# A four-layer residual kernel with two convolutions and two mixes: the prologue is rebuilt

## The chip, the cores and the metric

The kernel runs on one core of a Trainium2 chip. The metric is the device time in microseconds; the comparison is between medians of several executions of the kernel before and of the kernel after the change. One execution of each was also recorded by the profiler.

## What is computed

For 32 samples, each x of 128 channels by 2048 positions, and a condition vector of 128 for each sample:

```python
x = x + conv1d(x, w0, groups=4, taps=9, pad=4) + (cond @ ctx0.T)[:, :, None] + side[None, :, None]
for l in (1, 2):
    h = gelu(gelu(cond @ W0 + b0) @ W1 + b1)
    att = softmax(h @ W2 + b2)                      # 8 weights for each sample
    agg_w = einsum('bk,koi->boi', att, weight)      # a 128 x 128 matrix for each sample
    x = x + einsum('boi,bih->boh', agg_w, x) + (att @ bias_k)[:, :, None]
x = x + conv1d(x, w3, groups=4, taps=9, pad=4) + (cond @ ctx3.T)[:, :, None] + side[None, :, None]
```

## The kernel before, in words

The samples are worked on one after the other. A residual layer is a linear map plus the identity, so the identity is added to its weights. The two mixes of a sample are multiplied into one 128 x 128 matrix (`product`), which is applied once (`mix`). What remains for a sample is conv0 (layer 0), mix (layers 1 and 2) and conv3 (layer 3).

The positions of a sample are kept as four planes (`x_planes`: position modulo 4). A convolution is then 12 shifts, and each number is split in two parts (hi and lo) for precision; a shift needs three products: hi by hi, hi by lo, and lo by hi. That gives `TURNS` = 36 turns, and a turn (`conv_turns`, L677) is four matmuls of 32 rows by 512 columns, one for each group, side by side in the array. A mix is 12 such turns. The results of a sample fill four of the eight PSUM banks, and even and odd samples take turns at the halves.

For each sample, ScalarE writes the hi part (`high_x`, `high_y`, `high_z`) and VectorE the lo part (`low_x`, `low_y`, `low_z`). VectorE also sums the eight weights of each mix into the sample's matrices (`mix_matrices`, L526, 16 instructions), and splits their product (`split_product`). SP copies the split product to four places (`spread_mix_w`), loads x (`load_x`), copies the results of conv3 across partitions (`relay_out`) and stores them (`store`). GpSimd interleaves x into planes (`plane_x`) and the planes back into positions (`weave_out`). Order on an engine is that of the program; semaphores are the only waits across engines.

Step t (`one(t)`) does, on TensorE, conv0 of sample t, the first 18 turns of conv3 of sample t-1, the product of sample t+1, the other 18 turns, and the mix of sample t. ALL lists the 33 steps; a hardware loop runs steps 2 to 27 (`LOOP`, L225), the others are written out.

Ahead of the steps stands the prologue. It loads the weights, builds the taps of both convolutions as 128 x 128 matrices (`tap_blocks` on VectorE, L557, nine `tap_matmuls` on TensorE, L749, then `taps_high` and `taps_low`), computes the attention (`hidden`, `gelus`, `logits`, softmax on VectorE and ScalarE), spreads it to a table (`att_tab`), and computes the biases (`conv_biases`, L769, and `mixed_bias`, L762). In it are also conv0 of sample 0 and the first product. conv0 of sample 0 begins when x_lo and the low taps of sample 0 are there:

```python
            pe.wait_ge(taps_lo_done[0], PH)
            conv0(zero, range(MID))
```

Both products of samples 0 and 1 are written to a corner of bank 6, and the second waits behind the mix of 0:

```python
                if t.at(0):
                    product(t, 1)
                    pe.wait_ge(prod_lo_done, 2)
                    pe.wait_ge(taps_lo_done[1], PH)
```

## Time and profile before

| | us |
|---|---|
| median of 3 runs | 716.09 (715.66 to 717.77) |
| the profiled execution | 715.86 |
| its span | 714.1 |
| TensorE busy in the span | 664.8 |

The span is what the profiler sees of the execution, from the first instruction to the last; the profiled execution's own time is 1.8 us more. A time in the rows counts from the span's start. PE is TensorE, DVE VectorE, ACT ScalarE, POOL GpSimd, SP the queue from which most transfers are issued. "L683" is a line of the kernel. A time in square brackets is how long the engine had idled, and what ended that.

### The profile page before, as it was taken

The page shows a single profiled execution, that of the slowest core. Times are in us where ns is not written, and L with a number is a line of the kernel's source. Part 1 is how long each engine was busy: PE and PEld are TensorE (multiplying, and loading weights), DVE is VectorE, ACT ScalarE, POOL GpSimd, SP SyncE. Part 2 cuts the span into 40 slices and gives each one's busy share as a digit, 9 for nine tenths or more (in the row PEclk, how much of TensorE's full clock was granted, in tenths as well). Part 3 has the DMA queues.
Part 4 walks back from the last instruction along what each step waited for, and adds up shares of the span by engine and source line. Part 5 has one row for each costly group of instructions (what it writes and reads, how often), then busy time and mean ns, then how long its engine had stood idle before and what let it go on. Part 6 is the DMA issues. An engine that isn't in the chain of part 4 may idle for free.

```text
span 714.1 us, 24424 instructions
## 1 busy us (share of the span) xinstructions
PE 664.8 (93%) x11104; PEld 650.9 (91%) x11104; DVE 484.8 (68%) x941; ACT 256.5 (36%) x319; POOL 253.5 (36%) x94
## 2 busy tenths in 40 slices
PE   4846999999999999999999999999999999999970
PEld 4645889999999999999999999999999999999960
DVE  5378677767676667776777776787777777777221
ACT  3303433343334443434333444343443344432211
POOL 7022233343344444334334444433433444422220
PEclk9957999999999999999999999999999999999986
DMA  8131478889988888889998888888999888666666
GB/s 274 61 90 31 114 184 194 182 155 206 175 181 187 192 192 190 189 166 176 206 174 182 187 192 191 190 185 163 180 206 180 171 192 194 134 131 128 109 120 152
DMA packets 50238, 119.72 MB, mean 168 GB/s; under 512 B 5865, under 2 KB 25369, under 8 KB 42265
## 3 DMA queue, kind: packets, MB, share of 16 engines
q1 hardware_dynamic: 48592, 118.66, 77.7%
q10 hardware_dynamic: 1352, 0.57, 0.3%
q8 instruction: 22, 0.36, 0.3%
q14 instruction: 16, 0.12, 0.1%
q0 software_dynamic: 256, 0.01, 0.0%
HBM read 35.33 MB, written 33.55 MB: 96 GB/s over the span
## 4 chain that ended last, share of the span: by engine, by line
PE 91%; DVE 3%; DMA 2%; ACT 1%; issue 1%; ACTq 0%; SPq 0%; DVEq 0%
PE ps L683 77%; PE ps L724 12%; DMA out_planes<-in_L_cond_c_weight 1%; DMA out_planes<-out_taps 1%; DVE out_planes L561 1%; DVE acc L540 1%; PE ps L711 1%; PE ps L753 1%; DVE y_lo L503 0%; DVE z_lo L513 0%; DVE mat2T L540 0%; ACT out_sb L411 0%; PE ps L778 0%; DVE mat L540 0%; DVE taps_lo L569 0%
## 5 line engine op out<-in xcount | busy, mean ns | idle before, releaser
L337 POOL COPY out_sb<-out_planes 128x2048 f32<-128x2048 f32 x31 | 122.1, 3939 | 301.2 <-DMA out_planes<-out_taps 301.2
L683 PE MATMUL ps<-z_hi,taps_hi 32*128 32x512 f32 x1536 | 203.8, 402 | 3.6 <-DVE z_lo L513 3.6
L683 PE MATMUL ps<-x_hi,taps_hi 32*128 32x512 f32 x1536 | 202.2, 397 | 1.0 <-DVE prod L553 1.0
L683 PE MATMUL ps<-z_hi,taps_lo 32*128 32x512 f32 x1536 | 201.2, 394 | 0.5 <-issue 0.5
L683 PE MATMUL ps<-x_lo,taps_hi 32*128 32x512 f32 x1536 | 200.9, 394 | 0.0
L683 PE MATMUL ps<-x_hi,taps_lo 32*128 32x512 f32 x1536 | 200.7, 393 | 0.0
L683 PE MATMUL ps<-z_lo,taps_hi 32*128 32x512 f32 x1536 | 200.3, 393 | 0.0
L330 POOL COPY x_planes<-x_in 128x2048 f32<-128x2048 f32 x31 | 120.3, 3881 | 138.9 <-DVE x_lo L496 135.8
L388 ACT ACTIVATE y_hi<-ps,bias_tab 128x512 fp32r<-128x512 f32 x128 | 77.6, 690 | 213.5 <-PE ps L683 213.5
L513 DVE SCALAR_TENSOR_TENSOR z_lo<-ps,bias_tab,z_hi 128x1024 fp32r<-128x1024 f32 x64 | 79.2, 1280 | 74.9 <-ACT z_hi L398 74.9
L683 PEld LDWEIGHTS ps<-z_hi,taps_hi 32*128 32x128 f32 x1536 | 120.8, 186 | 6.1 <-DVE z_lo L513 4.0
L683 PEld LDWEIGHTS ps<-x_hi,taps_hi 32*128 32x128 f32 x1536 | 121.2, 186 | 3.0 <-DVE prod L553 1.2
L683 PEld LDWEIGHTS ps<-x_lo,taps_hi 32*128 32x128 f32 x1536 | 121.4, 187 | 1.7 <-issue 0.2
L683 PEld LDWEIGHTS ps<-x_hi,taps_lo 32*128 32x128 f32 x1536 | 121.3, 186 | 1.7
L683 PEld LDWEIGHTS ps<-z_lo,taps_hi 32*128 32x128 f32 x1536 | 121.1, 186 | 1.1
L683 PEld LDWEIGHTS ps<-z_hi,taps_lo 32*128 32x128 f32 x1536 | 120.6, 185 | 1.3
L503 DVE SCALAR_TENSOR_TENSOR y_lo<-ps,bias_tab,y_hi 128x512 fp32r<-128x512 f32 x128 | 87.3, 745 | 46.8 <-ACT y_hi L388 46.8
L724 PE MATMUL ps<-y_hi,mix_w 32*128 32x512 f32 x1024 | 98.9, 394 | 0.0
L406 ACT ACTIVATE out_taps<-ps,bias_tab 128x512 f32<-128x512 f32 x64 | 40.6, 685 | 155.7 <-PE ps L683 155.7
L398 ACT ACTIVATE z_hi<-ps,bias_tab 128x1024 fp32r<-128x1024 f32 x64 | 67.9, 1113 | 46.7 <-PE ps L724 46.7
L724 PEld LDWEIGHTS ps<-y_hi,mix_w 32*128 32x128 f32 x1024 | 72.8, 186 | 0.8
L496 DVE TENSOR_TENSOR x_lo<-x_planes,x_hi 128x2048 fp32r<-128x2048 f32 x31 | 70.8, 2285 | 0.0
(102 smaller groups left out, 566.2 us busy)
## 6 DMA issues: line engine op xcount, KB each, us to landing
out_planes<-out_taps SPq DMA_DIRECT2D x128, 256.0 KB, 7.4
x_in<-in_x SPq DMA_DIRECT2D x31, 1024.0 KB, 11.0
out<-out_sb SPq DMA_DIRECT2D x31, 1024.0 KB, 4.2
mix_w<-prod SPq DMA_DIRECT2D x128, 128.0 KB, 4.5
x_in<-in_x SPq DMA_DIRECT2D x2, 512.0 KB, 6.1
out<-out_sb SPq DMA_DIRECT2D x2, 512.0 KB, 3.1
out_taps<-in_L_cond_weight SPq DMA_DIRECT2D x1, 512.0 KB, 9.5
mix_w<-in_L_cond_weight SPq DMA_DIRECT2D x1, 512.0 KB, 13.2
```

The costliest lines, as they stand in the source:

```text
L330: pool.tensor_copy(x_planes[:, :, :], x_in[t.par(d)][:, :].rearrange("c (s p) -> c p s", p=PH))\
L337: pool.tensor_copy(out_sb[t.par(d)][:, :].rearrange("c (s p) -> c p s", p=PH), out_planes[:, :, :])\
L388: act.activation(y_hi[:, g, :], ps[:, bank(t, 0) + g, :], ACT.Identity, bias=bias_tab[:, b, g:g + 1]).then_inc(y_hi_done, 1)
L398: act.activation(z_hi[:, 2 * h:2 * h + 2, 1:S + 1], ps[:, k:k + 2, :], ACT.Identity, bias=bias_tab[:, b, 2 * G:BIAS]).then_inc(z_hi_done, 1)
L406: act.activation(out_taps[:, g, :], ps[:, bank(t, d) + g, :], ACT.Identity, bias=bias_tab[:, b, G + g:G + g + 1]).then_inc(out_act, 1)
L496: dve.tensor_tensor(out=x_lo[p][:, :, 1:S + 1], in0=x_planes[:, :, :], in1=x_hi[p][:, :, 1:S + 1].bitcast(F32), op=ALU.subtract).then_inc( ...
L503: dve.scalar_tensor_tensor(out=y_lo[:, g, :], in0=ps[:, bank(t, 0) + g, :], scalar=bias_tab[:, b, g:g + 1], in1=y_hi[:, g, :].bitcast(F32) ...
L513: dve.scalar_tensor_tensor(out=z_lo[:, 2 * h:2 * h + 2, 1:S + 1], in0=ps[:, k:k + 2, :], scalar=bias_tab[:, b, 2 * G:BIAS], in1=z_hi[:, 2 ...
L540: dve.scalar_tensor_tensor(out=o, in0=inputs[0], scalar=att_tab[:, b, K * l + k:K * l + k + 1], in1=inputs[1], op0=ALU.mult, op1=ALU.add). ...
L561: dve.tensor_copy(blocks[rows(g), :, rows(g)], conv_in[l][rows(g), :, :].rearrange("o c t -> o t c"))\
L683: tile = pe.matmul(ps[:, first_bank + g, :], w[rows(g), d, :], a[rows(g), d % PH, d // PH:d // PH + S], start=(n == 0), stop=(n == TURNS - 1))
L724: tile = pe.matmul(ps[:, bank(t, 0) + p, :], w[rows(p), g, h, :], a[rows(p), g, :], start=(n == 0), stop=(n == 3 * G - 1))
```

## The change

It touches only the prologue and the first steps; the arithmetic that gives the output is the same.

- **Loads.** SP issues both halves of x of sample 0 first, then the weights in the order of their use, and the x of sample 1 last. ScalarE issues conv0's taps, cond and four bias rows. The biases and `side` come as five rows and are turned by TensorE together with cond.
- **Taps.** VectorE transposes the taps in 32 x 32 blocks (`turn_taps`); `tap_blocks` and `tap_matmuls` go away. Both `taps_high` and `taps_low` read SBUF.
- **Biases.** The context products are one for each convolution (`contexts`), their result is multiplied with a 0/1 table (`ctx_columns`), and one product for each convolution spreads it. `mixed_bias` sums its eight products in PSUM.
- **First samples.** Samples 0 to 3 are read straight from `x_in`, at every fourth word, without `x_planes` (`PLANED` = 4). Steps 1 to 3 have an order of their own on ScalarE, VectorE, SP and GpSimd (`early`).
- **Turn order.** In every convolution the turns run over the 12 shifts first with hi by hi, then lo taps, then lo data; conv0 waits for x_lo only ahead of turn 24. conv0 of sample 0 is cut into eight pieces with the small products between them.
- **Second product.** conv0 of sample 1 runs around the mix of 0 (22 turns ahead of it, 14 behind); then comes the product of 1, into the banks of z of sample 0, and conv3 of 0 waits for its sum.
- The loop begins at step 4.

```diff
-        LOOP = (1, (N - 4) // 2)
+        LOOP = (2, (N - 4) // 2)
...
-                sp.wait_ge(x_planed, b - 1)
+                if isinstance(b, int) and b - 2 < PLANED:
+                    wait(sp, x_lo_done, b - 1)
+                else:
+                    sp.wait_ge(x_planed, b - 1 - PLANED)
...
+            def early(t):
+                if t.has(-2):
+                    relay_out(t, -2)
+                    load_x(t, 2)
+                    store(t, -2)
+                spread_mix_w(t, 1)
...
-            sp.dma_start(conv_in[0], conv0_w).then_inc(conv_w_in[0], DMA)
             for h in range(2):
                 sp.dma_start(x_in[0][:, h * L // 2:(h + 1) * L // 2], x[0, :, h * L // 2:(h + 1) * L // 2])\
                   .then_inc(x0_halves[h], DMA)
+            for l, m in enumerate((mix1, mix2)):
+                sp.dma_start(mlp_w[l][0], m[0]).then_inc(hidden_w_in[0], DMA)
+            sp.dma_start(mlp_rows[4:5, :], side.rearrange("(a c) -> a c", a=1)).then_inc(mlp_rows_in, DMA)
+            for l, m in enumerate((mix1, mix2)):
+                sp.dma_start(mlp_w[l][1], m[2]).then_inc(hidden_w_in[1], DMA)
+            for l, w in enumerate((ctx0_w, ctx3_w)):
+                sp.dma_start(ctx_in[l], w).then_inc(ctx_w_in[l], DMA)
+            sp.dma_start(conv_in[1], conv3_w).then_inc(conv_w_in[1], DMA)
             sp.dma_start(mix2_in, mix2[6].rearrange("k o i -> o k i")).then_inc(mix2_arrived, DMA)
+            sp.dma_start(mix1_w[:, :, :], mix1[6].rearrange("k o i -> o k i")).then_inc(mix1_arrived, DMA)
             sp.dma_start(x_in[1][:, :], x[1]).then_inc(x_loaded[1], DMA)
-            sp.dma_start(mix1_w[:, :, :], mix1[6].rearrange("k o i -> o k i")).then_inc(mix1_arrived, DMA)
             zero = Step(0, 0)
             load_x(zero, 2)
+            spread_mix_w(zero, 0)
             load_x(zero, 3)
-            spread_mix_w(zero, 0)
-            for t in ALL:
+            spread_mix_w(zero, 1)
+            for t in ALL[1:PLANED]:
+                early(t)
+            load_x(ALL[PLANED - 1], 3)
+            load_x(ALL[PLANED - 1], 4)
+            for t in ALL[PLANED:]:
                 one(t)
...
+            act.wait_ge(x0_halves[0], DMA)
+            act.activation(x_hi[0][:, :, 1:1 + S // 2], planes(x_in[0], half(0)), ACT.Copy).then_inc(x0_high, 1)
             gelus(0)
...
             gelus(1)
+            act.activation(soft[0:1, 41:42], ones[0:1, 0:1], ACT.Exp).then_inc(exp_tables, 1)
+            for p in range(PH):
+                taps_high(1, p)
...
+            def turn_taps(l):
                 dve.wait_ge(conv_w_in[l], DMA)
+                dve.transpose(taps_raw[l][:, :, :], conv_in[l].rearrange("o c t -> o t c")).then_inc(taps_raw_step[l], 1)
+                dve.wait_ge(fold_done, 1)
+                dve.wait_ge(taps_raw_step[l], 1)
+                dve.tensor_tensor(out=taps_raw[l][:, PAD, :], in0=taps_raw[l][:, PAD, :], in1=fold[:, :], op=ALU.add)\
+                   .then_inc(taps_raw_step[l], 1)
...
+            def early(t):
+                if t.at(1):
+                    low_y(t)
+                mix_matrices(t, 1)
+                if not t.at(1):
+                    low_y(t)
+                split_product(t, 1)
+                if t.at(1):
+                    evac_out(t, -1)
+                low_x(t, 1)
+                if not t.at(1):
+                    evac_out(t, -1)
+                low_z(t)
...
+            turn_taps(0)
+            dve.wait_ge(condT_psum, 2)
+            dve.tensor_copy(mlp_col[:, :], ps[:, 6, 0:N + 5]).then_inc(condT_done, 1)
+            dve.wait_ge(halo_done, HALOS)
+            dve.wait_ge(x0_halves[1], DMA)
+            dve.tensor_copy(x_hi[0][:, :, 1 + S // 2:1 + S], planes(x_in[0], half(1))).then_inc(x_hi_done, 1)
+            dve.wait_ge(taps_zeroed, 4)
             for p in range(PH):
                 taps_low(0, p)
+            dve.wait_ge(x0_high, 1)
+            low_x0(0)
+            turn_taps(1)
+            dve.wait_ge(x_hi_done, 1)
+            low_x0(1)
             dve.wait_ge(logits_psum, 1)
...
+            low_x(zero, 1)
+            dve.wait_ge(bias_tab_done, 3)
             low_y(zero)
...
+            mix_matrices(zero, 1)
+            low_z(zero)
+            split_product(zero, 1)
+            for t in ALL[1:PLANED]:
+                early(t)
+            low_x(ALL[PLANED - 1], 2)
+            for t in ALL[PLANED:]:
                 one(t)
...
-                    d, k = n // 3, n % 3
-                    w, a = ((taps_hi[l], hi), (taps_hi[l], lo), (taps_lo[l], hi))[k]
+                    k, d = n // SHIFTS, n % SHIFTS
+                    w, a = ((taps_hi[l], hi), (taps_lo[l], hi), (taps_hi[l], lo))[k]
...
+                if t.at(1):
+                    pe.wait_ge(prod_summed, 2)
...
+            hidden(0)
+            pe.wait_ge(taps_hi_done[0], PH)
+            conv0(zero, range(3))
+            hidden(1)
+            conv0(zero, range(3, 8))
+            logits()
+            conv0(zero, range(8, SHIFTS))
...
+            conv0(zero, range(28, 32))
             pe.wait_ge(agg_done, 1)
             product(zero, 0)
+            conv0(zero, range(32, TURNS))
             mixed_bias()
+
+            pe.wait_ge(bias_tab_done, 3)
+            pe.wait_ge(prod_summed, 1)
+            conv0(first, range(22))
+            mix(zero)
+            conv0(first, range(22, TURNS))
+            product(zero, 1)
+            pe.wait_ge(taps_lo_done[1], PH)
```

## Rows read from the trace of the kernel before

**Rows 1.** The page: the chain of waits, share of each engine.

```profile
PE 91%; DVE 3%; DMA 2%; ACT 1%; issue 1%; ACTq 0%; SPq 0%; DVEq 0%
```

**Rows 2.** Stretches: busy us (x instructions) of each engine, granted clock, DMA share, GB/s.

```profile
17.27:33.40 16.13, 16.13 (x182) 12.77 (x180) 3.60 (x13) 4.13 (x12) 1.63 (x1) 1.00 0.20 75
33.40:64.20 30.80, 12.79 (x87) 11.24 (x86) 23.39 (x58) 9.82 (x12) 3.84 (x1) 0.65 0.18 52
64.20:70.00 5.80, 5.77 (x56) 4.64 (x60) 5.80 (x4) 0.00 (x0) 3.50 (x1) 0.51 0.36 93
107.50:681.30 573.80, 573.80 (x9968) 573.43 (x9961) 410.43 (x791) 217.47 (x260) 215.69 (x56) 1.00 0.85 178
```

**Rows 3.** TensorE's timeline: start, us, line, operation, what it waited for.

```profile
17.27 0.80 PE L683 MATMUL ps<-x_hi,taps_hi 32*128 32x512 f32 x4
...
24.06 1.08 PE L778 MATMUL ps<-out_planes,out_sb 128*128 128x32 f32 x8
...
62.76 0.50 PE L707 MATMUL ps<-mat2T,mat 128*128 128x128 f32 x2 [4.94 <-DVE mat2T L540]
64.23 0.80 PE L683 MATMUL ps<-x_hi,taps_hi 32*128 32x512 f32 x4 [0.97 <-DVE prod L553]
...
75.25 0.42 PE L683 MATMUL ps<-z_hi,taps_hi 32*128 32x512 f32 x4
```

**Rows 4.** VectorE's timeline, same columns.

```profile
8.77 1.08 DVE L604 COPY x_planes<-x_in 128x1024 f32<-128x1024 f32 x1 [1.32 <-DMA x_in<-in_x]
...
20.50 0.68 DVE L630 TENSOR_TENSOR spread<-soft,ident 32x512 f32<-32x512 f32 x1
...
32.66 2.73 DVE L503 SCALAR_TENSOR_TENSOR y_lo<-ps,bias_tab,y_hi 128x512 fp32r<-128x512 f32 x4 [4.28 <-ACT y_hi L388]
35.46 0.35 DVE L540 SCALAR_TENSOR_TENSOR acc<-mix_w,att_tab,ident 128x128 f32<-128x128 f32 x1
...
39.42 0.33 DVE L540 SCALAR_TENSOR_TENSOR mat2T<-mix_wT,att_tab,acc 128x128 f32<-128x128 f32 x1
...
43.95 5.24 DVE L561 COPY out_planes<-out_sb 32x288 f32<-32x288 f32 x4
...
55.99 2.43 DVE L569 TENSOR_TENSOR taps_lo<-ps,taps_hi 128x288 fp32r<-128x288 f32 x4 [5.14 <-ACT taps_hi L417]
...
64.09 2.29 DVE L496 TENSOR_TENSOR x_lo<-x_planes,x_hi 128x2048 fp32r<-128x2048 f32 x1
66.30 2.47 DVE L513 SCALAR_TENSOR_TENSOR z_lo<-ps,bias_tab,z_hi 128x1024 fp32r<-128x1024 f32 x2
...
80.03 0.69 DVE L548 TENSOR_REDUCE prod_sum<-ps 128x128 f32<-128x512 f32 x1 [1.11 <-PE ps L711]
```

**Rows 5.** ScalarE's timeline, same columns.

```profile
18.07 1.28 ACT L474 ACT_TABLE_LOAD   x1
...
53.72 2.25 ACT L417 ACTIVATE taps_hi<-ps 128x288 fp32r<-128x288 f32 x4 [16.59 <-PE ps L753]
...
57.94 2.12 ACT L398 ACTIVATE z_hi<-ps,bias_tab 128x1024 fp32r<-128x1024 f32 x2 [0.26 <-PE ps L724]
```

**Rows 6.** GpSimd's timeline, same columns.

```profile
44.15 3.84 POOL L330 COPY x_planes<-x_in 128x2048 f32<-128x2048 f32 x1 [25.25 <-DVE x_lo L496]
```

**Rows 7.** The page's DMA issues: count, KB each, median us to landing.

```profile
x_in<-in_x SPq DMA_DIRECT2D x31, 1024.0 KB, 11.0
...
mix_w<-prod SPq DMA_DIRECT2D x128, 128.0 KB, 4.5
x_in<-in_x SPq DMA_DIRECT2D x2, 512.0 KB, 6.1
```

**Rows 8.** The chain of waits in order of time: start, us, what.

```profile
98.73 0.46 issue
...
100.38 4.31 PE ps L683 x70
...
147.07 12.58 PE ps L683 x216
```

More of the change, by code:

```diff
@@ L282, in one @@
             def one(t):
-                if t.has(-2) and not t.at(N + 1):
+                if t.has(-2):
                     relay_out(t, -2)
@@ L286, in one @@
                     load_x(t, 4)
-                if t.has(-2) and not t.at(N + 1):
+                if t.has(-2):
                     store(t, -2)
@@ L433, in one @@
             def one(t):
-                if t.has(0) and not t.at(0):
+                if t.has(0):
                     high_y(t)
@@ L495, in low_x @@
                 dve.wait_ge(x_hi_done, b + 1)
-                dve.tensor_tensor(out=x_lo[p][:, :, 1:S + 1], in0=x_planes[:, :, :],
+                direct = isinstance(b, int) and b < PLANED
+                dve.tensor_tensor(out=x_lo[p][:, :, 1:S + 1],
+                                  in0=planes(x_in[p], slice(0, S)) if direct else x_planes[:, :, :],
                                   in1=x_hi[p][:, :, 1:S + 1].bitcast(F32), op=ALU.subtract).then_inc(x_lo_done, 1)
@@ L581, in one @@
                     mix_matrices(t, 1)
-                if not t.at(0) and t.has(0):
+                if t.has(0):
                     low_y(t)
@@ L591, in one, with early, low_x0 @@
                     low_z(t)
+            def early(t):
+                if t.at(1):
[8 more added lines that the diff above has]
+                if not t.at(1):
+                    evac_out(t, -1)
+                low_z(t)
+            def low_x0(h):
+                s = slice(1 + half(h).start, 1 + half(h).stop)
+                last = dve.tensor_tensor(out=x_lo[0][:, :, s], in0=planes(x_in[0], half(h)),
+                                         in1=x_hi[0][:, :, s].bitcast(F32), op=ALU.subtract)
+                if h == 1:
+                    last.then_inc(x_lo_done, 1)
@@ L607, in _ @@
+            dve.wait_ge(taps_zeroed, 4)
             for p in range(PH):
                 taps_low(0, p)
-            dve.wait_ge(halo_done, HALOS)
-            dve.wait_ge(x_planed, 1)
-            for h in range(2):
-                dve.wait_ge((x0_high, x_hi_done)[h], 1)
-                s = slice(h * S // 2, (h + 1) * S // 2)
-                half = dve.tensor_tensor(out=x_lo[0][:, :, 1 + s.start:1 + s.stop], in0=x_planes[:, :, s],
-                                         in1=x_hi[0][:, :, 1 + s.start:1 + s.stop].bitcast(F32), op=ALU.subtract)
@@ L666, in _ @@
-            dve.wait_ge(bias_tab_done, 3)
-            for t in ALL:
+            dve.tensor_tensor(out=mixed_sum, in0=agg[:, 0, :], in1=agg[:, 1, :], op=ALU.add).then_inc(mixed_step, 1)
+            dve.wait_ge(mixed_step, 2)
+            dve.wait_ge(mixed_psum, 1)
+            dve.tensor_tensor(out=bias_tab[:, 0:N, 2 * G], in0=ps[:, 5, 0:N], in1=mixed_sum, op=ALU.add)\
+               .then_inc(bias_tab_done, 1)
+            low_x(zero, 1)
+            dve.wait_ge(bias_tab_done, 3)
+            low_y(zero)
@@ L732, in one @@
             def one(t):
-                if t.has(0) and not t.at(0):
+                mid = TURNS - 4 if t.at(1) else MID
+                if t.has(0) and not t.at(1):
                     conv0(t)
                 if t.has(-1):
-                    conv3(t, -1, range(MID))
-                if t.has(1) and not t.at(0):
+                    conv3(t, -1, range(mid))
+                if t.has(1):
                     product(t, 1)
                 if t.has(-1):
-                    conv3(t, -1, range(MID, TURNS))
+                    conv3(t, -1, range(mid, TURNS))
                 if t.has(0):
                     mix(t)
-                if t.at(0):
-                    product(t, 1)
-                    pe.wait_ge(prod_lo_done, 2)
-                    pe.wait_ge(taps_lo_done[1], PH)
-                    pe.wait_ge(bias_tab_done, 3)
-            def tap_matmuls(l):
-                pe.wait_ge(blocks_step, blocks_seen(l))
-                pe.wait_ge(fold_done, G)
-                for k in range(TAPS):
-                    last = pe.matmul(ps[:, 4, GC * k:GC * k + GC], blocks[:, k, :], fold[:, :], start=True, stop=True)
-                last.then_inc(taps_psum, 1)
             def mix2_transposes(h):
@@ L802, in logits @@
                 last.then_inc(logits_psum, 1)
-            zero = Step(0, 0)
+            zero, first = Step(0, 0), Step(0, 1)
             pe.wait_ge(ident_step, 3)
@@ L824, in _ @@
             pe.wait_ge(spread_done, 1)
[L825 removed]
+            pe.wait_ge(mix2T_done, 1)
+            pe.matmul(ps[:, 4, :], ones[0:N, :], spread[:, :, :].rearrange("n m k -> n (m k)"), start=True, stop=True)\
               .then_inc(att_tab_psum, 1)
[L827 to L829 removed]
             mix2_transposes(1)
+            conv0(zero, range(16, 20))
+            contexts()
             pe.wait_ge(attT_done, 1)
```

317 lines of the change are left out of this document (155 added, 162 removed).

## The prediction

> **What bounds the kernel now.** I read the page's chain of waits first: it runs through TensorE for 91% of the span [rows 1]. Next the table by stretches. From 107.5 to 681.3 us TensorE is busy for the whole of 573.8 us at full clock, with the transfers at 0.85 of their engines [rows 2]: there nothing but TensorE's own work sets the time. From 33.4 to 64.2 us it is busy 12.8 of 30.8 us, at a mean granted clock of 0.65 [rows 2]. So time can be won only ahead of the loop, and what is to be forecast is one instant: when the first turn of the second convolution, conv3 of sample 0, starts. Before, that is at 75.25 us [rows 3], and 714.1 - 75.25 = 638.85 us follow it. By then TensorE must have done conv0(0), conv0(1), the mix of 0 and the small products. A turn (four products side by side) costs 12.58/54 = 0.233 us at full clock [rows 8]. From 64.2 to 70 us, at a granted clock of 0.51, 56 products took 5.77 us [rows 2], 0.41 a turn; I use 0.43 for one wholly at the lower of the two levels (1.2 against 2.4 GHz). Two convolutions and a mix are 84 turns, 19.6 us. The rest of the 75 us is start-up, waiting and a low clock.
>
> **Where the waiting is.** conv0(0) begins at 17.27. After it TensorE waits for the matrices of sample 0, which VectorE sums only after low_y (first of 16 at 35.46, last ends 39.75) [rows 4], and the product comes after them. VectorE then builds the second tap blocks in four copies, 5.24 us [rows 4], because GpSimd's copy of x_planes runs from 44.15 to 47.99 [rows 6]; only after these come the 18 tap products, the mix of 0, the matrices of 1, and conv0(1) at 64.23 [rows 3].
>
> **The change, followed to the new instant.** I take the queues in their new order and carry one clock through them. Prices are of the rows named; where before has no such operation I give both bounds.
>
> *Start.* The taps go through a block transpose on VectorE instead of a memset, copies and nine products. No row shows a transpose; the nearest are below it the 0.68 us for 512 elements (spread) and above it the 1.3 us of each tap-block copy under GpSimd's copy [rows 4]. I take 0.5 us for 288 elements, bounds 0.3 and 1.3; it ends by about 4.5 us, ahead of the data of x, so on l = 0 it costs nothing, and at 1.3 would still be hidden by them. The two halves of x now lead SP's queue, issued near 0.7 and 1.2 us; at 6.1 us to landing [rows 7] the second is there near 7.3 (before, its first use was at 8.77 [rows 4]). The row of side inputs follows two 64 KB weights in the same queue: about 7.9, bounds 7 and 9.5. VectorE's new wait for that row has the rounding of half 1 of x, the low taps and x_lo of sample 0 queued behind it, so a late row moves all that follows one for one. Then condT is copied, VectorE rounds half 1 of x (1.08 us, the strided copy at 8.77 [rows 4]) while TensorE does hidden(0). conv0(0) can start at about 9.6, bounds 8.5 and 11.5, since it no longer waits for x_lo or the low taps.
>
> *To the attention table.* (Pieces without a row here are read from the same timelines, to 0.1 us.) Three cold turns 1.3, hidden(1) 0.9, five cold turns 2.1, logits 0.8: logits at 14.7. ScalarE meanwhile does gelu(1) until 12.4, loads the exponential's table (1.28 [rows 5]) and turns the second taps into taps_hi(1), 2.25 us [rows 5]: free at 16.0, later than the maxima. Two exponentials 0.65, reciprocals to spread 1.43: 18.1. VectorE then does the low taps of conv3, 2.43 [rows 4], the two copies 0.9, two context columns 0.6 (new; bounds 0.4 and 1.2 by one or two matrix steps each): 22.1. The 16 matrix steps of sample 0 take 4.29 (35.46 to 39.75 [rows 4]): 26.4, agg copied 26.6. TensorE has by then 32 of 36 turns done by about 25.2, so it waits some 1.4 us; the chain is VectorE's. Gone are six of ScalarE's eight context repeats, six of ten context products, nine tap products for each convolution and the tap blocks. What they cost lay in the stretch that is now built anew, so I don't subtract them apart.
>
> *To the first mix.* Product of 0 by 27.1 (0.5, as at 62.76 [rows 3]), its sum and split 0.9, bias tables and mixed_sum 0.7. Behind the product TensorE does four turns and the eight mixed_bias products: 0.9 + 2.0 (eight such passes took 1.08 us [rows 3], sixteen 2.0) = 30.0; VectorE adds, 30.3. Here conv0(1) starts, in place of 64.23 [rows 3]: 22 turns, 5.1 us, 35.5. VectorE: low_x(1) 2.29, low_y(0) 2.73 [rows 4]: 35.3. The spread of the product lands near 34.8 (last of four issues about 30.3, 4.5 to landing [rows 7]). Mix of 0: 2.8, 38.3. All three arrive within 0.7 us, so a slip in any of them shows.
>
> *To conv3(0).* VectorE's 16 matrix steps of sample 1 end at 39.6; z_hi (2.12 [rows 5]) is there at 40.4; low_z 2.47 [rows 4]: 42.1. The product of 1 now goes to the banks that z leaves, so it waits for that: 42.45. conv3(0) waits for its sum, 0.69 [rows 4]: 43.2. TensorE ran out of turns at 41.6, so but for the product itself it waits about 1.3 us; behind this stand all of conv3 and the mix of 1, and ScalarE, VectorE and SP wait for those in turn. 75.25 - 43.2 leaves 32.0 us. The load of x1 is moved behind the weights of both mixes on SP: there before 20, used at 21. x2 is issued near 14.3 and at 11.0 us [rows 7] there before 31, when it is used.
>
> *Behind it.* In step 1 the matrices of 2 end with conv3's 32nd turn: 0.1 us. In steps 2 and 3 the queues have 1 us or more in hand. At step 4 the order changes: VectorE has low_x(5) between low_z(3) and the matrices. It waits for GpSimd's plane copy, 3.84 [rows 6], which waits for low_x(4). I get low_x(5) done 6.4 us after conv0(4) starts, matrices 4.3, low_y 2.73: 13.5, where the product is due at 12.6: 0.9 us lost once, and 0.2 for GpSimd's copy beside VectorE's. The short stop at the loop's entry (0.46 us [rows 8]) moves with it. Splitting the turn order by k instead of d leaves 144 products with 144 weight loads per convolution: nothing.
>
> **Sum.** Span 638.85 + 43.2 + 1.2 = 683.3. The profiled execution took 715.86 for a span of 714.1, 1.8 more: 685.1. The median shown is 0.2 above it: 685.3.
>
> A rule weighed against the direct reading of x: VectorE's subtraction now takes x at every fourth word. The strided copy did 1024 elements in 1.08 us, the dense subtraction 2048 in 2.29 [rows 4], so the stride costs nothing I can see. The Trainium skill ("SBUF — State Buffer", Door 1, on cachelines) says that crossing to a new 16-byte line is penalised and that four fp32 can be strided free. If the penalty applied here, that subtraction would double by its row, 2.3 us on the chain, giving 687.6; the copy's row agrees with the free reading.
>
> **Rivals.** *A: the start chain is longer.* Its cause would be a late side row, the clock, or VectorE's queue held. TensorE's waits from 33.4 to 64.2 us, 18 us in all, left it at 0.51 from 64.2 to 70 [rows 2], whereas soon after the 0.46 us stop 18 turns took 4.31 us, full clock [rows 8]. The stops of 1.4 and 1.3 us lie between these. A fall costs what the stretch from 64.23 to 75.25 shows: 36 turns in 11.0 instead of 8.4 [rows 3], 2.6 us each. With a start 1.9 late: 688 to 692. Chance 0.20. *B: shorter*, with earlier rows, full clock from 13 us, and no stop at step 4: 680 to 682.5. Chance 0.12. *C: it is given back ahead of the loop*, by SP's one queue: the load of x4 stands behind relay_out(0), the spread of 3 behind store(0), and that waits for GpSimd's weave. If these ran 10 us or more behind my clock, steps 2 to 4 would be held until the old pace is met, at most the whole 30.8: 693 to 716. Against it: the spread of 3 has some 20 us in hand, x4 some 15. 0.04. *D: slower.* The turn order is changed in all 64 convolutions, 2304 turns. If a new order cost 14 ns more per turn than 0.233, 32 us would be lost and the gain gone; at 20 ns it is 46 us, and the time 731. The mix, whose order puts other weights and tiles side by side, takes the same 2.8 us for 12, so I give it 0.02. The forecast itself, 682.5 to 688: 0.62.
>
> The range 680 to 691 holds forecast, B and most of A, 0.9 by my chances; its ends are the sums with the lower and upper bounds together. Faster by over 0.3% (about what a measurement here can tell from no change): all of A, B, the forecast, most of C: 0.95. Within: 0.02. Slower: 0.03.
>
> **What would show it.** conv0(0) starting near 9.6, the first matrix step near 22 and the product near 26.6 on TensorE, conv0(1) near 30.3, conv3(0) near 43.2; a wait of about 1.3 us ahead of conv3(0) on prod_sum; one of about 1 us at the product of step 4; turns at 0.233 in the loop. The prediction falls if a load (side row, weights) lands after 12 us, if the clock drops in the two waits, or if turns in the loop have another length.

## The result, and the profile after

The changed kernel takes 697.07 us (median of 4 runs, 695.89 to 698.2) against 715.88 for the kernel before: a ratio of 0.9736, interval 0.9707 to 0.9766. It is faster, as forecast, but 11.8 us above the forecast of 685.3 and outside its range. The profiled execution has a span of 695.3 us, where I had worked out 683.3; its own time is 697.07. So 12.0 us have to be found.

TensorE's timeline of the changed kernel, the instants of my clock (the lines answer to [rows 3]):

```profile
9.60 1.65 PE L755 MATMUL ps<-x_hi,taps_hi 32*128 32x512 f32 x12
...
12.17 2.50 PE L755 MATMUL ps<-x_hi,taps_hi 32*128 32x512 f32 x20
...
18.90 1.81 PE L755 MATMUL ps<-x_hi,taps_lo 32*128 32x512 f32 x16
...
22.23 1.21 PE L755 MATMUL ps<-x_hi,taps_lo 32*128 32x512 f32 x16
...
29.09 0.46 PE L787 MATMUL ps<-mat2T,mat 128*128 128x128 f32 x2 [0.84 <-DVE agg L716]
...
32.97 4.66 PE L755 MATMUL ps<-x_hi,taps_hi 32*128 32x512 f32 x48 [0.38 <-DVE bias_tab L728]
...
48.15 2.15 PE L755 MATMUL ps<-z_hi,taps_hi 32*128 32x512 f32 x32 [0.95 <-DVE prod_sum L592]
```

conv0(0) starts at 9.60, as forecast; conv3(0) at 48.15 instead of 43.2, which is 4.95 us of the 12.0. (That 9.6 comes out to the digit is chance: in the fifteen other traces with the new prologue conv0(0) starts between 9.8 and 10.6, in e14, the same kernel, at 10.18. All lie within the bounds of 8.5 to 11.5.) Behind conv3(0)'s start 647.15 us follow, where I had 638.85 + 1.2: 7.1 us more. In the list one also sees where the turns become quick: 16 products (four turns) take 1.81 us at 18.90 and 1.21 us from 22.23 on.

VectorE's timeline of the changed kernel ahead of conv3(0) (answers to [rows 4]):

```profile
17.94 2.45 DVE L612 TENSOR_TENSOR taps_lo<-taps_raw,taps_hi 128x288 fp32r<-128x288 f32 x4
...
20.80 0.21 DVE L703 COPY attT_sb<-ps 8x64 f32<-8x64 f32 x1 [0.41 <-PE ps L899]
21.75 0.69 DVE L706 COPY att_tab<-ps 128x512 f32<-128x512 f32 x1 [0.73 <-PE ps L903]
24.03 0.61 DVE L658 SCALAR_TENSOR_TENSOR out_sb<-ps,mlp_col,of_group 128x128 f32<-128x128 f32 x2 [1.60 <-PE ps L844]
24.56 0.35 DVE L584 SCALAR_TENSOR_TENSOR acc<-mix_w,att_tab,ident 128x128 f32<-128x128 f32 x1
...
32.80 3.92 DVE L537 TENSOR_TENSOR x_lo<-x_in,x_hi 128x2048 fp32r<-128x2048 f32 x1
36.62 2.72 DVE L545 SCALAR_TENSOR_TENSOR y_lo<-ps,bias_tab,y_hi 128x512 fp32r<-128x512 f32 x4
```

Three waits on TensorE, 0.41 + 0.73 + 1.60 us, put the first matrix step at 24.56 instead of 22.1. And the subtraction that reads x at every fourth word takes 3.92 us, not 2.29.

The same timelines, VectorE, GpSimd and TensorE, at the entry of the loop, step 4, whose conv0 starts at 100.86:

```profile
107.35 0.35 DVE L584 SCALAR_TENSOR_TENSOR acc<-mix_w,att_tab,ident 128x128 f32<-128x128 f32 x1
107.55 3.90 POOL L360 COPY x_planes<-x_in 128x2048 f32<-128x2048 f32 x1 [4.41 <-DVE x_lo L537]
107.61 3.99 DVE L584 SCALAR_TENSOR_TENSOR acc<-mix_wT,att_tab,ident 128x128 f32<-128x128 f32 x1
...
115.20 2.72 DVE L545 SCALAR_TENSOR_TENSOR y_lo<-ps,bias_tab,y_hi 128x512 fp32r<-128x512 f32 x4
...
117.97 0.81 PE L793 MATMUL ps<-mat2T,mat 32*128 32x128 f32 x8 [4.32 <-DVE y_lo L545]
```

One matrix step, usually 0.35 us, takes 3.99: it begins 0.06 us behind GpSimd's plane copy and ends just after that copy has (111.45). TensorE then waits 4.32 us for the product of sample 5. The table by stretches shows what comes with it (columns as in [rows 2]):

```profile
33.00:34.00 1.00, 1.00 (x16) 0.89 (x20) 1.00 (x1) 1.00 (x2) 0.00 (x0) 0.97 0.92 154
34.00:37.00 3.00, 3.00 (x32) 2.95 (x29) 3.00 (x2) 3.00 (x1) 0.00 (x0) 0.50 0.34 43
...
115.90:122.70 6.80, 4.73 (x48) 3.99 (x52) 5.72 (x8) 0.00 (x0) 3.90 (x1) 0.50 0.48 152
122.70:681.00 558.30, 550.55 (x9508) 540.97 (x9504) 394.73 (x742) 206.77 (x247) 207.11 (x53) 0.99 0.85 177
```

TensorE's granted clock is at half, 1.2 GHz, from 34 to 37 us and from 115.9 to 122.7. In all, the distance from conv0(4) to conv0(5) is 26.57 us, that from conv0(2) to conv0(3) 21.08, from conv0(5) to conv0(6) 20.69; then every step takes 19.77 to 19.79, up to the last ones.

### The profile page after: what moved, and what is told of

It reads as the page before. It is cut to its first block, busy times and chain, and to the rows that moved or that the text cites. A ratio compares the mean times of both kernels' runs of the same rounds, so it can differ in the third digit from the quotient of the medians.

```text
span 695.3 us, 24314 instructions
## 1 busy us (share of the span) xinstructions
PE 657.3 (95%) x11062; PEld 636.9 (92%) x11062; DVE 495.4 (71%) x931; ACT 261.6 (38%) x313; POOL 239.2 (34%) x89
## 4 chain that ended last, share of the span: by engine, by line
PE 91%; DVE 4%; DMA 2%; ACT 1%; issue 1%; SPq 0%; ACTq 0%; DVEq 0%
PE ps L755 76%; PE ps L806 13%; DMA out_planes<-out_taps 1%; DVE acc L584 1%; PE ps L793 1%; DMA out_planes<-in_fside_S 1%; DVE z_lo L555 1%; DVE x_lo L537 1%; ACT z_hi L440 0%; DVE y_lo L545 0%; DVE mat L584 0%; PE ps L863 0%; ACT out_sb L453 0%; PE ps L837 0%; ACT x_hi L424 0%
## 5 line engine op out<-in xcount | busy, mean ns | idle before, releaser
L755 PE MATMUL ps<-z_hi,taps_lo 32*128 32x512 f32 x1536 | 106.2, 402 | 0.6 <-issue 0.6
L755 PE MATMUL ps<-z_hi,taps_hi 32*128 32x512 f32 x1536 | 100.7, 399 | 4.7 <-DVE z_lo L555 3.7
L755 PE MATMUL ps<-x_hi,taps_hi 32*128 32x512 f32 x1536 | 102.3, 404 | 0.8 <-DVE out_taps L565 0.4
L755 PE MATMUL ps<-z_lo,taps_hi 32*128 32x512 f32 x1536 | 98.6, 393 | 0.4 <-issue 0.4
L755 PE MATMUL ps<-x_hi,taps_lo 32*128 32x512 f32 x1536 | 98.9, 391 | 0.0
L755 PE MATMUL ps<-x_lo,taps_hi 32*128 32x512 f32 x1536 | 98.5, 391 | 0.0
L755 PEld LDWEIGHTS ps<-z_lo,taps_hi 32*128 32x128 f32 x1536 | 89.7, 185 | 3.0 <-issue 0.8
L755 PEld LDWEIGHTS ps<-x_hi,taps_lo 32*128 32x128 f32 x1536 | 90.2, 185 | 1.5 <-issue 0.5
L755 PEld LDWEIGHTS ps<-z_hi,taps_lo 32*128 32x128 f32 x1536 | 88.9, 187 | 2.9 <-issue 1.1
L755 PEld LDWEIGHTS ps<-x_lo,taps_hi 32*128 32x128 f32 x1536 | 90.1, 183 | 1.2
L440 ACT ACTIVATE z_hi<-ps,bias_tab 128x1024 fp32r<-128x1024 f32 x64 | 67.9, 1112 | 52.5 <-PE ps L806 52.5
```

The source lines that it names most:

```text
L440: act.activation(z_hi[:, 2 * h:2 * h + 2, 1:S + 1], ps[:, k:k + 2, :], ACT.Identity, bias=bias_tab[:, b, 2 * G:BIAS]).then_inc(z_hi_done, 1)
L755: tile = pe.matmul(ps[:, first_bank + g, :], w[rows(g), d, :], a[rows(g), d % PH, d // PH:d // PH + S], start=(n == 0), stop=(n == TURNS - 1))
```

## The experiments

All ratios are against the kernel before on the same chip. In the text "the kernel after" is the changed kernel, 0.9736.

### The entry of the loop

**e1.** GpSimd holds the plane copy of sample 6 until the matrices of sample 5 are summed.

```diff
             def one(t):
+                if t.at(PLANED):
+                    pool.wait_ge(mats_step, 2 * K * (PLANED + 2))
                 if t.has(2):
                     plane_x(t, 2)
```

> GpSimd's plane copy of sample 6 waits until VectorE has summed the matrices of sample 5; nothing else differs from the changed kernel. Theory (the two engines' common way to SBUF): the one matrix step that took 3.99 us beside that copy takes 0.35, TensorE waits about 0.7 us instead of 4.3 ahead of the product in step 4, its clock does not fall there (2.3 us more), so about 6 us less: 691. Rival (VectorE is simply late by low_x of sample 5, the copy only fills its time): the wait stays near 4 us and the time at 697.

**e2.** Step 3 gets the order of the loop instead: low_x(4) ahead of low_y(3), and sample 5 planed early.

```diff
-                low_x(t, 1)
+                low_x(t, 2 if t.at(PLANED - 1) else 1)
...
-            low_x(ALL[PLANED - 1], 2)
```

> Step 3 takes the loop's order: x of sample 5 is loaded ahead of relay_out(1), low_x of 4 goes ahead of low_y of 3, the planes and high part of 5 follow at once, and low_x of 5 is done in step 3. Theory: the wait of 4.3 us at the product of step 4 and the clock's fall behind it go away, 6 to 7 us less, 690 to 691; at most 0.5 us is lost in step 3. Rival (the wait moves one step ahead): a wait of 2 us or more in step 3, 693 to 697.

Measured: e1 699.08 us, ratio 0.9759 (0.9724 to 0.9793); e2 698.07, 0.9789 (0.9738 to 0.9839). In both the stall is gone: at the product of step 4 TensorE waits 0.62 us in e1, and step 4 takes 20.70 us there and 19.86 in e2. e2 pays for it in step 3, as its rival said in part: 21.65 us for 19.83, since conv0(4) waits for VectorE's evacuation. So the cause of the 4.32 us is settled, and yet neither kernel is faster. The last conv0 starts 2.0 and 4.4 us sooner than in the kernel after (640.74 and 638.42 against 642.78), but the tail behind it is 56.7 and 56.5 us instead of 52.5. (In e1 the gain of TensorE is larger than these 2.0 us. Its recorded execution reached conv0(2) 2.5 us late, at 62.41, for reasons that the edit doesn't touch: among them a granted clock of 0.57 from 49 to 53 us. From conv0(2) to the last conv0 it is 4.5 us shorter than the kernel after.) The end of e1's chain of waits shows what sets the tail:

```profile
658.07 3.88 POOL out_sb L366
661.95 12.52 issue
674.47 3.87 POOLq L54
...
681.95 8.81 DMA out_planes<-out_taps
```

It is no longer TensorE but a ring of waits: SP issues the relay of the results, 8 to 9 us later they are there, GpSimd weaves them in 3.9 us, SP stores, and only then is `out_planes` free for the next relay. Whoever speeds TensorE up ahead of the loop meets this ring at the end. Its first weave starts at 71.54 in the kernel after and its second interval is 25.3 us; in SP's queue two loads of x stand ahead of relay 2, and e9 tests whether that is why.

**e9 and e10.** SP's queue at the loop's entry in another order: the load of sample 6 right behind that of 5, relay 2 ahead of the load of 7; e10 is this with the hold of e1.

```diff
                     load_x(t, 2)
+                    if t.at(PLANED - 1):
+                        load_x(t, 3)
                     store(t, -2)
...
-            load_x(ALL[PLANED - 1], 3)
-            load_x(ALL[PLANED - 1], 4)
...
                     relay_out(t, -2)
+                if t.at(PLANED):
+                    load_x(t, 3)
```

> Same work in another order on the SyncE queue: the load of sample 6 stands right behind that of sample 5 in step 3, and the relay of output 2 ahead of the load of sample 7. Theory R (the relay-weave-store ring has no time to spare at the entry of the loop, and the weaves 1 and 2 lie 25.3 us apart because the relay waits behind two loads): the gap shrinks to 21.5 to 23.5 us, the relay being issued at about 101.2 instead of 103.6; but TensorE's step 4 stays near 26 us, since GpSimd's plane copy of sample 6 then comes even sooner and still holds up the matrices of sample 5; total 694 to 697. Rival (the gap is set by TensorE's own late step, not by the queue): gap stays at 25 and nothing moves.

> The same, and GpSimd holds the plane copy of sample 6 until the matrices of sample 5 are there. Theory R: step 4 of TensorE about 20.7 us as with the hold alone, weave 2 starts at about 117.8 instead of 120.5, so that the ring gains 2 to 3 us against the hold alone, and the total is 693 to 697. Rival (the ring is not what took the gain of the hold): the tail stays at 56 to 57 us behind the last first convolution and the total at 697 to 700.

Measured: e9 699.65, ratio 0.9777 (0.9761 to 0.9794); e10 693.78, 0.9699 (0.9683 to 0.9715). In e9 the second interval of the weaves fell to 20.4 us, so the loads were its cause, but step 4 grew to 30.09, where I had expected 26: the weave now came at 113.47, right behind the plane copy (108.22), and held a second matrix step, 3.75 us long; TensorE waited 7.71 us for the product. With the hold (e10) the second interval is 23.2 us, the tail 52.2, and the kernel is the first one below the kernel after. Step 4 is 22.55, where I had expected 20.7: conv0(5) now waits 1.68 us for VectorE's evacuation.

**e13, e14, e15.** All three on one chip: e14 is the kernel after, unchanged, e15 is e10 again, and e13 adds to it that weave 2 waits until the product of 5 is split, and that VectorE evacuates ahead of low_x in steps 2 and 4.

```diff
+                if t.at(PLANED):
+                    pool.wait_ge(prod_lo_done, PLANED + 2)
                 if t.has(-2):
                     weave_out(t, -2)
...
-                if t.at(1):
+                if t.i <= 2:
                     evac_out(t, -1)
                 low_x(t, 1)
```

> The order of queue entries of the ninth and tenth edits (SyncE order, GpSimd holds the copy of sample 6), and besides: GpSimd's weave of output 2 waits until the product of sample 5 is split, and VectorE evacuates output 1 ahead of the subtraction of sample 3 in step 2 and output 3 ahead of that of sample 6 in step 4. Theory: what is left of the entry's delay is a VectorE cast held beside a GpSimd weave (1.5 us in step 2, 3.8 us in step 4), which makes the evacuation, and so the next first convolution, late. Then step 2 is 19.8 to 20.0 instead of 20.9, step 4 20 to 20.9 instead of 22.55, and the total 690.0 to 693.0. Rival (the ring takes it back): TensorE's steps shrink so, but the tail behind the last first convolution grows from 52 to 55 or more and the total stays at 693.5 to 696.

> The changed kernel as it is, on the same chip, as the measure for the two others: 695.5 to 698.5.

> The tenth edit again beside the unchanged kernel. Theory: 693 to 694.5, that is 2.5 to 4 us below it, by step 4 at 22 to 23 us instead of 26.6 and a tail of 52 us. Rival: the lead of the tenth run was scatter from chip to chip, and the two lie within 1.5 us.

Measured: e14 698.1 us, ratio 0.9758 (0.9742 to 0.9774); e15 694.31, 0.9704 (0.9689 to 0.972); e13 694.32, 0.9698 (0.9683 to 0.9713). So the lead of e10 over the kernel after is real, 3.8 us on one chip, with intervals that do not touch; it is that of the queue order and the hold together, since neither e9 nor e1 has it alone. e13 did to TensorE nearly all that was asked. Against e15, step 2 takes 20.03 us instead of 20.90, step 4 20.69 instead of 22.56 and step 5 19.77 instead of 21.41; step 3 lost 1.0 us (20.85 for 19.83), since its product waits for y_lo. The last conv0 starts at 636.60, 3.3 us ahead of e15. And the time did not change: the tail grew from 52.8 to 56.3. The ring took it, as the rival said. From 200 to 640 us the waits of e13 name it (engine, line, what it waited for: us in all, times, longest):

```profile
ACT out_taps L454 <- DMA out_planes<-out_taps: 82.7, 17, 5.2
...
DVE out_taps L571 <- DMA out_planes<-out_taps: 17.4, 17, 1.4
```

In the kernel after, the first of these waits was on TensorE.

**e6, e7, e8.** The ring shortened where it seemed cheapest: SP spreads the next product before it waits for the weave, not after the store; in e7 with the hold of e1, in e8 with the order of e2.

```diff
+                if t.has(1):
+                    spread_mix_w(t, 1)
                 if t.has(-2):
                     store(t, -2)
-                if t.has(1):
-                    spread_mix_w(t, 1)
```

> SP's queue spreads the next product ahead of the store that waits for GpSimd's weave, in every step from 1 on; nothing else differs from the changed kernel. Theory of two bounds (TensorE with its stall in step 4, and beside it the ring relay_out, landing, weave, store, spread, relay_out, which takes 19.8 us a step and so never makes up what it lost in steps 1 to 3): the ring falls to some 16 us, but TensorE still stalls 4.3 us in step 4 and its clock falls, so the time stays within 1.5 us of the changed kernel's, 695.5 to 698. Rival (the ring alone decides): 690 to 692.

> The spread ahead of the store, and GpSimd's plane copy of sample 6 held back until VectorE has summed the matrices of 5. Theory of two bounds: both are lifted, so the 5.8 us that step 4 gained when the copy was held back now reach the end: 690 to 692, the last conv0 starts near 636.5 and the end follows it by 52.5 us. Rival (the gain in step 4 is lost for another reason, as more transfers at once): 696 to 699.

> The spread ahead of the store, and step 3 in the loop's order. Theory of two bounds: 689 to 691.5, since the last conv0 started at 638.4 us with step 3's order alone and the tail was 4 us longer than TensorE needs; the 1.6 us wait in step 3 for VectorE's evacuation stays. Rival: 696 to 698, as step 3's order alone.

Measured: 704.25 (ratio 0.9821, 0.9796 to 0.9847), 699.46 (0.9762, 0.9745 to 0.9779), 701.28 (0.9807, 0.9778 to 0.9836). The tail is TensorE's again (51.7 to 52.5 us), but the loop's steps, 19.78 before, now take 19.8 to 20.4. The weave starts a little earlier in each step and lies on VectorE's cast. From 240 to 620 us the groups of e7:

```profile
L598 DVE CAST prod<-prod_sum 128x128 fp32r<-128x128 f32 x19 | 40.9, 2155 | 0.6
```

A cast of 0.23 us takes 2.16 on average, in every step, the evacuation behind it is late, and TensorE waits for its bank. In the kernel after the same cast averages 0.72 us and nothing waits. In e1 a matrix step takes the blow instead (2.13 us on average), and there it costs little, since the product is seldom due yet: e1's steps average 19.88 us. What a GpSimd copy costs depends on which instruction of VectorE it meets.

**e12.** That price by itself: at the very end of the kernel five more plane copies, beside each of them one kind of operation.

```diff
+                    if k == 6:
+                        dve.wait_ge(beside_done, i + 1)
...
+                        op().then_inc(beside_step, 1)
```

> The unchanged kernel, and at its very end five rounds in which GpSimd makes one more plane copy (128x2048) while VectorE runs four evacuations from PSUM, then one kind of operation of 128x128 twice, and after the copy twice more. Theory G (a VectorE operation whose operands all lie in SBUF is held until GpSimd's copy has ended, one that reads PSUM is not): the first cast, subtraction, scaled sum and addition of a constant beside the copy each take what is left of the copy (some 0.5 to 1.5 us), the sum that reads PSUM takes its usual time of about 0.35. Rival (only the cast or only forms with a scalar are held): one or more of the four take their usual 0.25 to 0.35 beside the copy.

Four operations of each kind, the first two meant to lie beside the copy, the last two behind it (min/median/max in ns):

```profile
L755 DVE CAST x_lo<-prod_sum x4: 227/227/786, 692.4 to 693.8; 128x128 fp32r<-128x128 f32 x4
...
L756 DVE TENSOR_TENSOR x_lo<-prod_sum,prod x4: 291/292/847, 697.4 to 699.0; 128x128 fp32r<-128x128 f32 x4
...
L757 DVE SCALAR_TENSOR_TENSOR mat<-mix_w,att_tab,ident x4: 352/352/848, 702.7 to 704.4; 128x128 f32<-128x128 f32 x4
...
L759 DVE TENSOR_SCALAR out_taps<-out_planes,bias_tab x4: 286/286/784, 708.2 to 709.6; 128x128 f32<-128x128 f32 x4
...
L760 DVE SCALAR_TENSOR_TENSOR y_lo<-ps,bias_tab,y_hi x4: 351/351/352, 713.3 to 714.5; 128x128 fp32r<-128x128 f32 x4
```

Each of the first four kinds has one operation of 0.78 to 0.85 us: the first, which is held for the rest of GpSimd's copy. The fifth, with one operand in PSUM and one in SBUF, started beside the copy as well and took its 0.35. The evacuations that ran under the copies were not stretched either, and GpSimd's copies took 3.81 us each. (The run took 717.21 us, its span is 715.4; about 20 us of it are the added work.)

### Ahead of conv3(0)

**e4.** Reads at strides of 1, 2, 4 and 8 words, 256 elements, at the end of the kernel.

```diff
+            dve.tensor_tensor(out=x_lo[0][:, 1, 0:256], in0=xf[:, 0:512:2], in1=hf, op=ALU.subtract)
+            dve.tensor_tensor(out=x_lo[0][:, 2, 0:256], in0=xf[:, 0:1024:4], in1=hf, op=ALU.subtract)
...
+            act.activation(x_lo[1][:, 2, 0:256], xf[:, 0:1024:4], ACT.Copy)
```

> Behind all work VectorE subtracts and copies, and ScalarE copies, 256 words read at a stride of 1, 2, 4 and 8 words; the outputs stay the reference's. Theory (a read at every fourth word costs VectorE's two-input subtraction and ScalarE about twice a dense one, the copy on VectorE no more than one word a cycle): subtraction 0.3 us dense and 0.5 at 4, ScalarE 0.35 and 0.6, copy 0.17 dense and 0.3 at 4. Rival (the direct reads were slow because two engines read x_in at once): equal times at strides 1 to 4. Whether 8 costs more than 4 is open: twice again if every new line is paid by its distance, the same if only the crossing counts.

```profile
687.99 0.41 DVE L753 TENSOR_TENSOR x_lo<-x_planes,x_hi 128x256 fp32r<-128x256 f32 x1
688.33 0.41 DVE L754 TENSOR_TENSOR x_lo<-x_planes,x_hi 128x256 fp32r<-128x256 f32 x1
688.65 0.60 DVE L755 TENSOR_TENSOR x_lo<-x_planes,x_hi 128x256 fp32r<-128x256 f32 x1
...
689.18 0.43 ACT L532 ACTIVATE x_lo<-x_planes 128x256 fp32r<-128x256 f32 x1
689.18 0.60 DVE L756 TENSOR_TENSOR x_lo<-x_planes,x_hi 128x256 fp32r<-128x256 f32 x1
689.51 0.66 ACT L533 ACTIVATE x_lo<-x_planes 128x256 fp32r<-128x256 f32 x1
```

A stride of 2 words is free, 4 and 8 cost the same: 0.60 against 0.41 us for the subtraction, 0.66 against 0.43 for ScalarE. VectorE's cast went from 0.27 to 0.38. At its full length the subtraction has a larger ratio, 3.92 against 2.29 us, 1.7 times. The execution took 695.35 us.

**e11.** Sample 1 read without the stride, which leaves out the order of its phases.

```diff
-                    src = planes(x_in[p], slice(0, S))
+                    src = x_in[p][:, :].rearrange("c (p s) -> c p s", p=PH) if b == 1 else planes(x_in[p], slice(0, S))
```

> Leaves out the order of the phases of sample 1: ScalarE and VectorE read its row without a stride, so that its values stand at other places, and the two passes cost what a dense pass costs. Theory S (the stride of four words costs 1.6 us on the path ahead of the first second convolution): the subtraction takes 2.29 instead of 3.92 us, ScalarE's copy 1.94 instead of 3.92, and the second convolution of sample 0 starts at 46.2 to 46.9 instead of 48.15. Rival (something else ends last there, the terms of the bias or TensorE's low clock): the subtraction is 1.6 us shorter and the second convolution starts where it did, within 0.5 us.

Measured: 696.11 us, ratio 0.9754 (0.9713 to 0.9795). The subtraction took 2.28 us, and from conv0(1) to conv3(0) there are 13.64 us (34.13 to 47.77) instead of 15.18, so 1.54 less. Not all of it is the stride's: in e11 the granted clock also stayed at 1.00 through conv0(1), where the kernel after fell to half (stretches above). e9 has the stride and a clock that stayed up, and takes 14.85 for the same distance:

```profile
33.83 3.15 PE L757 MATMUL ps<-x_hi,taps_hi 32*128 32x512 f32 x48 [0.38 <-DVE bias_tab L730]
...
40.25 0.51 PE L808 MATMUL ps<-y_hi,mix_w 32*128 32x512 f32 x4 [0.94 <-DVE y_lo L547]
```

Like with like, the stride costs 1.2 us of the path (14.85 to 13.64), and the clock's fall 0.3. The instant of conv3(0) itself moved only by 0.38, since the stretch up to the first matrix step, which this edit doesn't touch, was 1.2 us later (25.75 for 24.56).

**e5.** Sample 1 goes through GpSimd's planes, so that the reads are dense and correct.

```diff
+            pool.wait_ge(x_loaded[1], DMA)
+            pool.tensor_copy(x_planes[:, :, :], planes(x_in[1], slice(0, S))).then_inc(x1_planed, 1)
```

> GpSimd copies sample 1 into planes as soon as it is loaded; ScalarE and VectorE read it dense. Theory (a read at every fourth word costs VectorE 3.92 us instead of 2.29, and that lies on the way to conv3 of 0): low_x of 1 takes 2.3 us and VectorE's matrices of 1 end 1.6 us earlier, but the mix of 0 waits for TensorE's own 22 turns, at low clock in part, so conv3 of 0 starts at most 0.5 us earlier, and the time stays at 696 to 697.5. Rival (VectorE alone sets conv3 of 0): 1.6 us earlier. GpSimd's copy beside VectorE may cost up to 1.6 us between 14 and 20 us.

Measured: 697.81 us, ratio 0.9738 (0.9712 to 0.9763). The subtraction was down to 2.28 us, and from conv0(1) to conv3(0) there are 13.63 us, as in e11: a second witness for the price of the stride. But conv0(1) started at 37.98 instead of 32.97 and conv3(0) at 51.61. Beside GpSimd's copy (15.39 to 19.28) a softmax instruction of VectorE of 0.22 us took 1.92, and TensorE's turns stayed at 0.43 us until about 32 us; what kept them slow I can't say.

**e3.** TensorE gets 16 products of the identity while the first loads are under way.

```diff
             pe.wait_ge(ident_step, 3)
+            for _ in range(16):
+                pe.matmul(ps[:, 0, 0:C], ident[:, :], ident[:, :], start=True, stop=True)
```

> TensorE multiplies the identity by itself 16 times into a bank that conv0 of 0 clears later, before it waits for the first loads; results are not used. Theory (the turns of conv0 of 0 ran at 1.2 GHz until about 22 us for want of earlier work): the first turns at 9.6 us take 0.23 us each instead of 0.43 to 0.5, and conv3 of 0 starts 2 to 4 us earlier: 693 to 695. Rival (the start chain is VectorE's and the loads', TensorE's rate does not matter): conv3 of 0 within 0.5 us of 48.15, time 697.

Measured: 697.16 us, ratio 0.9729 (0.9699 to 0.976): no gain. conv0(0) started at 10.29 and conv3(0) at 48.38. The stretches of e3, and two pieces of its conv0(0):

```profile
10.00:15.00 5.00, 4.71 (x38) 3.17 (x38) 4.89 (x8) 2.99 (x9) 0.00 (x0) 0.59 0.95 312
15.00:20.00 5.00, 5.00 (x38) 3.67 (x40) 4.23 (x12) 2.55 (x9) 0.00 (x0) 0.50 0.51 197
```

```profile
15.61 2.08 PE L755 MATMUL ps<-x_hi,taps_hi 32*128 32x512 f32 x16
...
22.74 1.22 PE L755 MATMUL ps<-x_hi,taps_lo 32*128 32x512 f32 x16
```

The granted clock is recorded at half from 15 to 20 us and 16 products take 2.08 us. In the kernel after a piece of 16 takes 2.08 us at 15.42 too, though its record says 1.00 there. I infer from the equal durations that both ran at the lower level; the record alone does not say so. When the turns become quick varies from trace to trace, between 19.5 and 23.5 us (22.2 in the kernel after, 19.9 in e14, which is the same kernel; in e5 about 32). What would lift the clock sooner I did not find.

## Why the forecast was too low

The 12.0 us divide so: 2.5 up to the first matrix step, 0.2 from there to conv0(1), 2.3 from conv0(1) to conv3(0), and 7.1 behind it.

**Up to conv0(0): right.** The start at 9.6, the side row, the logits (15.4 for 14.7) and the spread (18.0 for 18.1) stood, the logits' 0.7 us being hidden. One price was off without harm: the block transposes, 0.69 and 0.72 us for 0.5.

**"To the attention table": failed, 2.5 us.** I let the chain be VectorE's from 18.1 on. It was TensorE's: between the logits and the contexts it has 48 products of conv0 and the transposes, the first 32 of them at 0.45 to 0.52 us a turn. VectorE's three waits on it are 2.74 us. I had carried the cold price only up to the logits. e3 shows the same durations with the clock recorded at half. That the chain is TensorE's is read from these waits; no run takes its products away. What the clock's share is, the other traces show: where the turns were quick by about 20 us (e2, e4, e7, e10, e12, e14), the first matrix step came 14.2 to 14.5 us behind the start of conv0(0); where they were quick only at 22 us or later (the kernel after, e1, e3, e6, e8, e9, e11, e15), 14.8 to 15.5. For the same kernel it is 14.44 (e14) and 14.96. The forecast had 12.5. So some 0.5 us of the 2.5 go with a late rise of the clock, and the rest is there even where it rises early. From there conv0(1) was 2.67 us late (32.97 for 30.3), with the matrices' own 4.3 us as forecast.

**The stride: failed, 1.6 us in the subtraction, 1.2 us of them on the path.** The step "the stride costs nothing I can see" compared a strided copy with a dense subtraction, two kinds of operation with different rates. e4 prices it at 1.5 times for 256 elements of the same operation, the kernel itself at 1.7 times for 2048, and e11 and e5 against e9 show 1.2 us of it on the path. I had weighed the rule of the Trainium skill ("SBUF — State Buffer", Door 1) and took its "four fp32" and my row for a sign that it is free. The traces agree with the page's other sentence, that a line wants at least two hits: 2 words free, 4 and 8 equally dear. My figure for a penalty, a doubling (2.3 us), was too high: it is 1.6.

**The clock in conv0(1), rival A: in part.** From 34 to 37 us the granted clock was at half, after waits of 0.84 and 0.38 us and the small products between them, and 48 products took 4.66 us. e9, where it stayed up, took 3.15 for them and then waited 0.94 us for y_lo, which the strided subtraction had delayed. So the fall and the stride cover each other, and the fall itself cost only about 0.3 us: 15.18 against 14.85 us from conv0(1) to conv3(0). It doesn't come each time: seven of the sixteen traces with the new prologue have it there, and of e10 and e15, which are the same kernel, only e10. In three others (e1, e3, e8) the clock fell at conv3(0) instead, where 48 products took 4.62 us for 3.09; with it conv0(2) came 13.3 us behind conv3(0) for 11.8, 1.5 us that the kernel after was spared. What decides between these I can't say. The last 0.7 us ahead of conv3(0) are small handovers: from the mix to conv3(0) there are 8.3 to 8.4 us in all traces, for 7.7 in my sum.

**Behind conv3(0): failed, 7.1 us.** I gave 0.2 us for GpSimd's copy beside VectorE's and 0.9 for the queue at step 4. The term for the queue at step 4 was right (e1, with the copy held, waits 0.62 us there); the 0.2 for the copy, which no row supported, is the term that failed. Step 4 lost 6.8 us against 19.8: one matrix step held for a whole copy (3.6 us), the queue's own 0.7, and the half clock that came with this wait, under which 4.7 us of work up to 122.7 cost about 2.4 too many. Step 2 lost 1.3 us to a cast held beside weave 0 (1.68 us) and to the strided subtraction (3.85 us) ahead of the evacuation; with the evacuation first (e13) it takes 20.03. Step 5 lost 0.9, of which 0.64 us is a stop of TensorE for which the trace names no wait; the kernel before had such a stop, 0.46 us, in its step 2 (20.49), so this one was moved and not added. The steps of the loop are as forecast, 19.78, and the turn order costs nothing (12.57 us for 54 turns): rival D is refuted. Rival C had 693 to 716 us, and 697.07 lies in it, but not by its mechanism: none of TensorE's lost time here is a wait for x4 or for the spread. Something given back through SP's queue has another place than I gave it: it is the ring of relay, weave and store, which stood unseen behind TensorE and took back what e1, e2 and e13 gained.

The Trainium skill has the rule ("SBUF — State Buffer", Who interferes with whom): an instruction of VectorE with two SBUF inputs, or in a two-port mode, and a GpSimd instruction that reads SBUF exclude each other for the whole of the first. All five kinds of e12 agree. I had not weighed it, and [rows 4] with [rows 6] had a case of it, which my prediction misread as 1.3 us for each of the four tap-block copies (5.24 in all) beside GpSimd's copy, 44.15 to 47.99. One of them took nearly all of it, in the kernel before:

```profile
44.40 3.87 DVE L561 COPY out_planes<-out_sb 32x288 f32<-32x288 f32 x1
```

The other three took 0.42 to 0.43 us. By that rule the question for step 4 would have been which instruction starts while the plane copy runs, and the answer was on my own clock.

Not settled: why the clock stays low up to 19.5 us and more in all versions, what makes it fall in one execution and not in another, and whether the ring and TensorE can both be served. The best version, e10 (e15 is the same), beats both kernels, with ratios of 0.9699 and 0.9704; e13, at 0.9698, is its equal.

## What to carry to other kernels

Price a strided read only against the same operation without a stride, and a cold engine up to the instant at which its rows show it quick, not up to the next milestone. Where GpSimd copies in SBUF, lay its copies over the instructions of VectorE one by one: here those that read PSUM passed, and casts, copies, sums and subtractions with all operands in SBUF were held to the copy's end, and what that costs depends on who waits for the one that is hit. And where a stall is removed and the time stays, look at the tail: a second ring, here relay, weave and store, can take as long as the engine that seemed to set the pace. And compare an instant in two traces only from the last instant in which they agree: here the start alone scatters by more than 1 us.

## What the runs showed of the hardware

- A VectorE operation of 0.23 to 0.35 us with all its operands in SBUF took 1.68 (kernel after), 2.16 (e7, mean of 19) or 3.99 us (kernel after) beside a GpSimd copy, and a copy of 0.43 us took 3.87 (kernel before); with an operand in PSUM it took its usual time (0.35, e12). ScalarE's x_hi took 1.94 us beside a copy and 1.93 without.
- Strides of 4 and 8 words cost VectorE's subtraction 0.60 against 0.41 us and ScalarE 0.66 against 0.43 for 256 elements; 2 words cost nothing.
- The recorded granted clock and the length of products can disagree: 16 products took 2.08 us in the kernel after with 1.00 recorded, and in e3 with 0.50 recorded; at the full level they take 1.21.
- The same program does not always keep the same clock: 48 products in conv0(1) took 4.62 us in e10 and 3.16 in e15, which are the same kernel; in all, 4.6 in seven traces and 3.15 or 3.16 in nine.
- Sixteen identity products on TensorE, which kept it busy from 1.7 to 8.2 us, ahead of the small ones, did not keep the clock up (e3): it is recorded at 0.59, 0.50 and 0.88 in the three stretches of 5 us from 10 us on.
